# Two squares added by an accumulating DMA, and the result's accumulating DMA issued earlier on GpSimd

## What is computed

```python
def layer(x, ...):
    # first norm, then the mixer
    omega_scaled = (x @ W_omega.T + b_omega) * exp(log_scale) / sqrt(position)
    phi = cumsum(omega_scaled, axis=1)
    cm_real, cm_imag = x * cos(phi), x * sin(phi)
    mem_real = cumsum(cm_real, axis=1) / position
    mem_imag = cumsum(cm_imag, axis=1) / position
    ret_real = mem_real * cos(phi) + mem_imag * sin(phi)
    ret_imag = mem_imag * cos(phi) - mem_real * sin(phi)
    context = concatenate([cm_real, cm_imag, ret_real, ret_imag])
    h = layernorm(context) * gamma + beta          # needs the sum of all squares
    h = gelu(h @ W1.T + b1) @ W2.T + b2
    return x + h

x = x + layer(layernorm(x), ...)
x = x + (relu(layernorm(x) @ ternary(W1).T + b1) @ ternary(W2).T + b2)
```

## Time and profile before

| | |
|---|---|
| median of 3 runs | 1531.16 us (1529.48 to 1537.38) |
| profiled execution | 1533.96 us, its span 1532.2 us |
| TensorE busy | 1470.5 us, 96% |
| VectorE busy | 1438.2 us, 94% |
| ScalarE busy | 1253.4 us, 82% |
| GpSimd busy | 616.9 us, 40% |
| mean granted TensorE clock | 0.991 of full speed |
| DMA queue of GpSimd, share of the 16 engines | 34.3% |
| DMA queue of SP, share of the 16 engines | 18.4% |

### The profile page before, as it was taken

How to read it: one execution, slowest core, us unless ns; L and a number is a source line. 1 busy time by engine, 2 the same in 40 slices (tenths; PEclk the granted TensorE clock), 3 DMA queues, 4 the chain that set the end, 5 groups by cost and what they waited for, 6 DMA issues and landing times.

```text
span 1532.2 us, 29929 instructions
## 1 busy us (share of the span) xinstructions
PE 1470.5 (96%) x10685; PEld 878.0 (57%) x10685; DVE 1438.2 (94%) x2325; ACT 1253.4 (82%) x1773; POOL 616.9 (40%) x393
## 2 busy tenths in 40 slices
PE   3779999999999999999999999999999999999998
PEld 2445566656555665555665655566565566555556
DVE  7999999999999999999999999999999999989954
ACT  6768888888988888988888898888888788888756
POOL 1333444433354443444444334444344444334331
PEclk9899999999999999999999999999999999999999
DMA  6325545555645655654555564455565455555452
GB/s 219 67 58 111 102 80 109 108 111 113 123 76 100 111 104 111 124 107 79 105 111 110 111 125 94 83 111 103 109 125 109 73 109 111 110 111 101 73 90 42
DMA packets 231427, 158.20 MB, mean 103 GB/s; under 512 B 138608, under 2 KB 221552, under 8 KB 231280
## 3 DMA queue, kind: packets, MB, share of 16 engines
q0 software_dynamic: 59376, 83.37, 34.3%
q1 hardware_dynamic: 170272, 69.25, 18.4%
q10 hardware_dynamic: 1632, 3.67, 0.7%
HBM read 24.13 MB, written 33.03 MB: 37 GB/s over the span
## 4 chain that ended last, share of the span: by engine, by line
DVE 35%; PE 24%; issue 14%; ACT 12%; POOL 7%; DMA 4%; SPq 2%; DVEq 1%; ACTq 0%; POOLq 0%
PE ps L966 11%; DVE arena L1332 5%; POOL sqr L535 4%; DVE arena L1400 4%; PE ps L1000 4%; PE ps L987 4%; POOL sqr L537 3%; PE ps L1021 3%; ACT xs L601 3%; DVE mr L1285 3%; ACT base L581 3%; DVE arena L1361 2%; DVE bn L1170 2%; DVE arena L1356 2%; DVE qb L1316 2%
## 5 line engine op out<-in xcount | busy, mean ns | idle before, releaser
L966 PE MATMUL ps<-arena,w_hi 128*128 128x512 f16 x2048 | 609.2, 379 | 3.0 <-DVE arena L1332 1.6
L966 PE MATMUL ps<-arena,w_lo 128*128 128x512 f16 x1024 | 388.3, 379 | 0.0
L966 PEld LDWEIGHTS ps<-arena,w_hi 128*128 128x128 f16 x2048 | 197.5, 98 | 224.2 <-issue 2.0
L987 PE MATMUL ps<-turned,fw_t 128*128 128x512 f16 x1024 | 250.6, 380 | 8.6 <-DMA turned<-rows 4.1
L1000 PE MATMUL ps<-fw_t,arena 128*128 128x256 f16 x2048 | 255.0, 273 | 1.9 <-DVE arena L1400 1.9
L1000 PEld LDWEIGHTS ps<-fw_t,arena 128*128 128x128 f16 x2048 | 197.8, 97 | 63.8 <-issue 16.7
L704 ACT ACTIVATE arena<-ps,relu_bias,relu_scale 128x512 f32<-128x512 f32 x256 | 197.0, 769 | 24.8 <-PE ps L987 24.4
L535 POOL TENSOR_TENSOR sqr<-sqr,turn 128x1024 f32<-128x1024 f32 x32 | 84.3, 2635 | 323.3 <-DVE arena L1332 323.3
L1400 DVE TENSOR_TENSOR arena<-arena 128x512 f16<-128x512 f32 x256 | 172.0, 681 | 19.5 <-ACT arena L713 17.5
L1021 PE MATMUL ps<-w_hi,arena 128*128 128x256 f16 x1024 | 172.9, 273 | 0.3 <-issue 0.3
L966 PEld LDWEIGHTS ps<-arena,w_lo 128*128 128x128 f16 x1024 | 100.0, 98 | 121.0
(11 more groups left out here) (189 smaller groups left out, 2850.4 us busy)
## 6 DMA issues: line engine op xcount, KB each, us to landing
x_rows<-in_L_attn_x SPq DMA_DIRECT2D x32, 512.0 KB, 6.5
rr<-qa POOLq DMA_DIRECT2D x32, 512.0 KB, 6.2
ri<-qb POOLq DMA_DIRECT2D x32, 512.0 KB, 9.0
base<-bias_rows POOLq DMA_DIRECT2D x32, 512.0 KB, 5.5
x<-bias_rows POOLq DMA_DIRECT2D x32, 512.0 KB, 5.5
out<-x SPq DMA_DIRECT2D x31, 512.0 KB, 7.6
out<-x POOLq DMA_DIRECT2D x31, 512.0 KB, 11.2
arena<-in_L_attn_W ACTq DMA_DIRECT2D x1, 2048.0 KB, 11.8
```

What stands on the lines that cost most here:

```text
L966: last = pe.matmul(ps[:, 4 + m], w[:, k, m * P:(m + 1) * P], a[:, c.b, k], start=(i == 0), stop=(i == len(passes) - 1))
L987: last = pe.matmul(ps[:, 4 + m % KE], fw1_t[:, k, m * P:(m + 1) * P], a[:, k], start=(i == 0), stop=(i == len(passes) - 1))
```

## The change

`square_sums` no longer adds the two squares on GpSimd. It issues an accumulating DMA, sqr += turn, as soon as both squares are there, waits until it has landed, and only then waits for cl_done[3]; the fold at line 537 stays. q2_done is now counted in sixteens. And `output_sum(before)` is called directly behind `inverse_std_2(now)`, not behind `retrieve(ahead)`.

```diff
                 if now:
                     inverse_std_2(now)
+                if before:
+                    output_sum(before)
                 if nxt:
                     square_lo(nxt, ahead)
...
                 if ahead:
                     product_imag_sin(ahead)
                     retrieve(ahead)
-                if before:
-                    output_sum(before)
                 if ahead:
                     square_sums(ahead)
 
             def square_sums(c):
                 need(pool, sqr_done, c)
                 need(pool, sqi_done, c)
+                pool.dma_start(sqr[:, :, :], turn[:, :, :], accum_op=ALU.add).then_inc(q2_done, 16)
+                need_sum(pool, q2_done, c)
                 need(pool, cl_done[3], c)
-                pool.tensor_tensor(sqr[:, :, :], sqr[:, :, :], turn[:, :, :], ALU.add).then_inc(q2_done, 1)
-                need(pool, q2_done, c)
                 pool.tensor_tensor(sqr[:, 0], sqr[:, 0], sqr[:, 1], ALU.add).then_inc(q_done, 1)
...
             def whole_turns(c):
                 need(act, y_done, c)
-                need(act, q2_done, c, 1)
+                need_sum(act, q2_done, c, 1)
```

## The result

| | kernel before | changed kernel |
|---|---|---|
| median, same comparison | 1533.26 us (1529.48 to 1537.38, 4 runs) | 1518.57 us (1517.85 to 1519.34, 4 runs) |
| profiled execution, span | 1533.96 us, 1532.2 us | 1519.01 us, 1517.2 us |
| mean granted TensorE clock | 0.991 | 0.992 |

The ratio is 0.9907, 95% interval 0.9883 to 0.9932: faster by 0.9%, some 15 us. The forecast was 1522.0, range 1517 to 1536.

A forecast was written before the change was run, and what follows sets the result against it. It took TensorE's matmuls as the floor, with VectorE making their inputs late. Steady waits 8.5, late step 1.4 and start-up 1.8 sum to 11.7 us: 1533.96 - 11.7 = 1522.3, set at 1522.0 for the median, range 1517 to 1536.

The forecast's parts named there:

- TensorE's floor: Steady steps at line 939: 44.85 us of matmuls without a wait, against 45.21 each over 26 steps.
- likeliest case: Whole kernel: the forecast of 1518 to 1523.5 us, chance 0.50.
- The steady waits: TensorE's waits over 26 steady steps: 8.5 of 9.3 us go, as VectorE gains 1.4 us of room per step.
- The late step: One step of 49.98 us, 5.1 over the floor, its transposes 3.0 late: 1.4 us go.
- The start-up: Before the first full step, the scan pair at 63.30 takes 2.5 for 4.40 us: 1.8 us gained.
- The scans' reading: VectorE's line 1237 loses about what GpSimd's lines 535 and 537 hold; 2.5 for 4.15 us, 1.6 per step.
- Line 535 as a DMA: GpSimd's 32 additions of 2.64 us become transfers issued behind the second square, landing after 7 us.
- 10.5 us bound: Ahead of line 537: from this landing time on, the addition's DMA makes the kernel slower; rival's chance 0.10.
- (b): GpSimd's queue behind the moved result's issue, held 0.9 us: nothing on the path, 0 to 0.3 us per step without cover.
- The transposes' meeting: Rival: the moved result's data and x1_bias slow the transposes at 756.7, giving 1536 to 1548 us; chance 0.07.

The follow-up runs named there:

- the first part alone: Changed kernel with the result's accumulating DMA back behind the ri issue, the squares still added by DMA: 1522.98 us, ratio 0.9924.
- One place further on: Result's DMA issued behind line 478 instead of ahead of line 544: changed kernel so edited 1519.11 us; the same with GpSimd adding the squares 1542.66 us.
- the unread addition: Changed kernel plus a GpSimd addition of 128x1024 behind the fold, its result read by nobody: 1556.94 us, ratio 1.0146.
- The early addition: Changed kernel with GpSimd adding the squares instead of the DMA, still ahead of the wait for cl_done[3]: 1529.16 us, ratio 0.9969.
- The pow of 128x4: Changed kernel plus a GpSimd power on 128x4 elements behind the fold, its result read by nobody: 1518.37 us.

## Why the prediction was right, and where its terms were off

- **TensorE's floor.** 44.85 us a step, read off one step without a wait, held in all 29. This bound is why the time came out inside the likeliest case. With line 1180 short again (1519.11) or no addition at all (1517.92) the time is the same.
- **The steady waits, 8.5 of 9.3 us.** All 9.3 went. Waits of 1.0 us against 1.4 us of lead was the argument. The lead that was won is 5.40 - 4.50 = 0.9 us, for the reason below; no wait over 0.2 is left all the same. Slow transposes haven't gone: SP's issue rows of 5.9 to 6.3 us still come, at 124.27, 258.98, 528.06, 662.77 and 932.13 among others, and TensorE doesn't wait behind them.
- **The late step, 1.4 of 5.1 us.** Mis-sized: all 5.1 went. In the trace of before, TensorE waited 2.96 us for line 446's transposes at 1364.21, and the granted clock stood at 0.73 and 0.84 between 1362 and 1370 us, so the step lost more than its wait. The wait came from a transposing DMA that itself landed late, as line 446's landings over the whole run of the kernel before show:

```profile
DMA to landing us min/median/max: 2.4/2.5/6.4
```

A landing 3.9 us late is more than the lead covers, and in the steady part of the changed kernel's two profiles no landing of that line took over 4.1 us. That the change prevents it isn't shown, so the 3.7 us above the forecast's 1.4 are luck as far as the two profiles go. What the runs show is the spread: 1526.85 to 1544.8 in 43 runs of the kernel before, 1517.77 to 1519.34 in both sets of the changed one.
- **The start-up, 1.8 us.** 0.56 came in one profile of the changed kernel and 1.87 in the other. In both the scan pair fell from 4.40 to 2.46 us. The sign matmuls of line 1108, last to wait for VectorE's chain there, begin at 97.37 before, at 95.43 in the second profile, 1.94 earlier, as forecast, and at 96.02 in the first, which was already 0.6 late at the program's first line 939 (74.81; 74.22 in the second, 74.23 before). The first then loses 0.8 more in a stretch at half clock, shown below. So the size was right for what the change gives, and an execution can keep back most of it.
- **The scans' reading.** The prediction has them lose about what lines 535 and 537 hold. They lost 1.8 us (4.15 for 2.33) beside 3.1 us of these two rows (741.11 to 744.18), of which line 537's own standing still is 0.8 (2.06 for 1.26). The 1.6 us per step was right; the two holds don't simply add up.
- **Line 535 as a DMA.** Issue directly behind the second square: right (ScalarE's line 661 ends at 727.93 in that step, the issue row begins at 728.46). Landing 7 us: 5.3 was the median of the whole run, 5.9 in the window; right side of the 10.5 us bound, and the fold released by VectorE in 27 of 32. What a landing near 9.2 does, which the prediction called harmless, the first part alone shows: 9.1 us, long scans in 20 steps of 32, and 3 to 4 us lost.
- **The moved issue, (b), "nothing".** Its size was wrong. I counted what is queued behind it on GpSimd and who waits for that, and found room; I did not ask which VectorE instruction line 544 would then stand beside. It costs VectorE 1.3 us a step. In the changed kernel this is hidden behind TensorE; alone it is part of a loss of 32 us, where the text had 0 to 0.3 us per step. It is also why VectorE comes to line 1337 at 750.55, 0.6 us behind TensorE's line 945 (749.95), and does not idle there as forecast.
- **The transposes' meeting.** No sign in the changed kernel (turned<-rows 2.5 us). One place further on the transposes are slowed in both kernels, and it costs time only without the lead.
- **The other landings.** rr took 8.2 us for 6.3. The new transfer isn't the cause: over the whole run rr took 7.8 us in the changed kernel and 7.9 without the transfer (6.2 before). What is, no run shows. ScalarE's line 633, which reads rr and ri, waited 0.8 us at most for rr, and for ri 9.6 us in 24 times where it had been 30.4 in 25: nothing was lost.

The exclusion rule of the Trainium skill, "SBUF — State Buffer", section "Who interferes with whom", has the shared pair held for a whole instruction by whoever is first. By that the scans lose what GpSimd's reader takes, and the unread addition agrees: 2.35 us on GpSimd, the pair at 4.39 for 2.33. The early addition agrees as well, in the other order (4.05 for 2.35 on GpSimd): its row begins at 733.25 inside VectorE's line 1361 (731.93 to 733.34), and it waits through lines 1400 and 1332 too, which follow without a gap. The pow of 128x4 doesn't: held for its 1.03 us, the scans would have ended 1 us later, and they took 2.35. The measurement decides; for so small an operand there is nothing to be feared here. The same section lists `tensor_scalar` among the instructions that can take both port pairs, when its operands meet conditions; line 1180 is one, and at 1.56 us beside line 544 it behaves so.

## What to carry to other kernels

When one engine is at 96% and another at 94%, take the floor of a step from a step without waits: it says how much all edits together can bring, here 14.4 us in the steady part, before any of them is costed. When an instruction moves, look not only at who waits for it but at what runs beside it on the engine that shares its ports: the same issue cost 32 us in one place, 11 one instruction further on, and nothing in either once the other engine had a lead. And a transfer that replaces work must be issued as far ahead of its use as the data allow; issued some 6 us later, it made this kernel 113 us slower.

## What the runs showed of the hardware

A 128x4 VectorE instruction can stand still behind a GpSimd instruction: line 1180 took 0.17 us where it stood clear of line 544 (128x512) or began in its last 0.1 us, 0.23 us where it began 0.2 us before line 544's end, as in most steps of the kernel before, and mostly 1.56 to 1.58 beside nearly the whole of it, in the changed kernel and six of its relatives, each time ending within 0.05 us of it. In the start-up of the kernel before it took 2.36 us: its row began 0.64 us ahead of line 544's (72.24 and 72.88) and still ended with it. So which of two rows begins first doesn't tell which instruction is held.

The squares' accumulating transfer, 512 KB from tile to tile, landed after 4.5 us (median of 32) when issued late and behind nothing, after 5.3 in the changed kernel, and after 8.6 behind the result's. The result's took 6.0 us in the new place and 11.6 in the old. The Trainium skill, "DMA: Bandwidth & Descriptors", section "Anatomy of one DMA — SWDGE (gpsimd) path", has a fit of 2.0 us plus bytes over 436e3 per transfer, which by estimate would be 3.2 us for 512 KB; the lowest median of these transfers is 4.5.

At the start the place of a stretch at half clock decides how much of an earlier input is kept. TensorE's windows in the kernel before and in the two profiles of the changed one, in that order (us of the window, PE busy, granted clock, DMA share, GB/s):

```profile
94.00:96.00 2.00, 0.00 (x0) 0.52 0.73 140
96.00:98.00 2.00, 0.63 (x7) 0.50 1.01 170
...
100.00:102.00 2.00, 2.00 (x16) 0.78 1.13 293
```

```profile
94.00:96.00 2.00, 0.00 (x0) 0.58 1.10 187
96.00:98.00 2.00, 1.98 (x19) 0.50 1.05 152
...
100.00:102.00 2.00, 2.00 (x8) 0.71 1.05 210
```

```profile
94.00:96.00 2.00, 0.57 (x6) 0.50 1.05 176
...
98.00:100.00 2.00, 2.00 (x16) 0.72 1.17 307
```

TensorE stood idle for 4.2 us before line 1108's sign matmuls in all three, and is granted 0.50 of its full clock, that is 1.2 GHz for 2.4, behind it. The windows' means put the end of that stretch near 100.9 us in the kernel before, 101.2 in the first profile and 99.1 in the second. So the work at half clock is 3.5 us long before (from 97.37), 5.1 in the first profile (from 96.02) and 3.7 in the second (from 95.43). The first profile's 1.6 us more at half speed are 0.8 us of time, which is what it lost; the second kept 1.87 of its 1.94. The same kernel can thus give up 0.8 us of an earlier input or nearly none, by where the stretch ends.
